# A decoder layer on one core: a unit's weighted values in one step of TensorE, ahead of the products with Wo

## The chip, the cores and the metric

The kernel runs on one core of a Trainium2 chip. The metric is the device time of one execution in microseconds (us). The kernel before took 1291.42 us, the median of three runs (1290.22 to 1291.81). Lower is better.

## The reference

`x` and `ctx` are (8, 256, 1024) float32, that is 8 sequences of 256 tokens. One layer is computed:

```python
qkv = x @ w_qkv                       # 32 query heads, 8 key and 8 value heads of 32
xq, xk = rope(xq), rope(xk)           # four query heads share one key and value head
probs = softmax(where(causal, xq @ xk.T / sqrt(32), -inf))
x = layernorm(x + (probs @ xv) @ w_o)
Q, K = x @ Wq.T + bq, ctx @ Wk.T + bk
x = layernorm(x + softmax(Q @ K.T / sqrt(1024)) @ ctx)
w = dequant_4bit(qweight, lut4)       # bit planes and a table of 16 values a row
x = layernorm(x + x @ w.T + bias)
```

(The third part also has an 8-bit weight for rows whose norm is over 64; rows of a layer norm over 1024 elements have a norm of 32, so the kernel computes the 4-bit product alone.)

Every large product is made from three matmuls: each operand is split into a high part (rounded by ScalarE) and a low part (the difference, by VectorE or GpSimd), and high x high, low x high and high x low are added up.

## The kernel before

There are five stages. Stage 1 (the first 210 us) computes the rotated queries and keys of three groups of 512 tokens in "pairs" of 48 matmuls, the values, and decodes on VectorE the first row blocks of the 4-bit weight; TensorE turns each decoded block (`turn_f`, eight transposes). Stage 2 (210 to some 665 us) is the self attention with the product with Wo. Then come the folding of Wq and Wk, the cross attention and the 4-bit product. The change is in stages 1 and 2.

Stage 2 runs over 8 batches (sequences). A batch is 24 steps (`SUB`), written out by hand on each engine in the same order; batches 0 and 1 stand on their own (age 0 and 1), batches 2 to 7 are a loop (age 2). A unit is one key head with its four query heads and takes three steps. The first two steps hold two heads each, of the later 128 queries against 256 keys; the third holds four heads of the first 128 queries against 128 keys. What happens to the scores of one step, engine by engine:

- TensorE: `scores` (L779) into a bank of PSUM.
- VectorE: `maxima`, masking and the row maximum, head by head (L1562).
- ScalarE: `exponent` (L1187), head by head.
- VectorE: the reciprocal of the sums (L1570), then GpSimd: `scale_probs` (L1907).
- TensorE, three steps later (`LAG`): `turn_probs` (L794, L805), four transposes into one of two banks.
- The copy of that bank to `probT`: by ScalarE for the first and third steps of a unit (L1117 in `probs_out`), by VectorE for the second (L1578). On ScalarE the copy stands behind the exponent of the step that it is in (from batch 1 on).
- TensorE, five steps later than the scores (`PV_LAG`): `weighted` (L818), the product of probabilities and values, in tiles of 32 columns.
- VectorE: the result to `att` (L1587). ScalarE and VectorE split `att`, and TensorE multiplies by Wo one batch later, four matmuls (128x512) in each step (`project_step`, L870).

TensorE's order in a step is: scores, four matmuls with Wo, weighted values, transposes. In batch 0, where no `att` of an earlier batch exists, about 30 matmuls of the last group's queries, keys and values (`fill`) take the place of those with Wo. The weighted values of a unit were issued in two parts: the 8 matmuls of its first two steps in a first step of a later unit (L834) and the 4 matmuls of its third step in the following, a second step (L838). The trace holds two records for each of these matmuls, so 16 and 8.

Each engine works strictly through its own list of instructions. VectorE's list for a second step of a unit is: maxima, reciprocal, copy of `probT`, copy of `att`, and at steps 4 and 16 of a batch the normalising of a 128x1024 tile (L1612, `NORM_STEP`); then the maxima of the third step follow. The tables `WO_STEPS`, `STEPS_OF`, `F_TURN` name the steps at which the parts of Wo are split, parts of the decoding are done and decoded blocks are turned. SyncE issues all DMAs in one order: the load of a unit's queries, keys and values stands behind the stores of the rotated last items (`store_item`).

## Time and profile before

| | |
|---|---|
| median of three runs | 1291.42 us |
| the profiled execution, own time | 1288.92 us |
| its span in the profile | 1287.1 us |
| TensorE matmul busy | 1263.6 us (98%) |
| VectorE, ScalarE, GpSimd busy | 901.6, 531.4, 477.2 us |
| granted TensorE clock | 0.999 |

Matmuls overlap in the records (a 128x512 matmul is recorded with 390 ns and the next starts 230 ns later), so a busy TensorE is read here from where one matmul starts to where the next one does. In rows of a view by time, x4 means that four instructions of one line in a row are shown as one, from the start of the first to the end of the last.

### The profile page before, as it was taken

The numbers are of one execution on the slowest core, as the hardware profiler recorded it, in microseconds if no ns is written. First come the engines' busy times: TensorE is split into PE (matmuls) and PEld (weight loads), VectorE is DVE, ScalarE is ACT, GpSimd is POOL, SyncE is SP. The second block draws the span as 40 slices with busy tenths as digits, with TensorE's granted clock in tenths as the row PEclk, the third lists the DMA queues.
The fourth block names the chain that finished last, engine by engine and source line by source line (L and its number), as shares of the span: only waits on it lengthen the run. The fifth ranks groups of instructions, "written<-read, shape, count | busy, mean of one in ns | idle before, by whom it ended". The sixth has DMA issues, their size and how long they took to land.

```text
span 1287.1 us, 25356 instructions
## 1 busy us (share of the span) xinstructions
PE 1263.6 (98%) x8230; PEld 1041.7 (81%) x8230; DVE 901.6 (70%) x2526; ACT 531.4 (41%) x1597; POOL 477.2 (37%) x413
## 2 busy tenths in 40 slices
PE   8999999998999999999999999999999999999997
PEld 6887888997777777777777887888888888888886
DVE  7999898578888888888876974353443636556665
ACT  4131212457777777777760223243433433100110
POOL 3512122345656656656550000544334450222221
PEclk9999999999999999999999999999999999999999
DMA  7165435463864344344343215125251419212221
GB/s 280 68 213 170 144 132 203 141 208 113 236 182 120 118 134 127 114 135 134 121 127 106 68 34 173 41 82 181 66 196 64 149 49 358 100 65 98 98 87 60
DMA packets 135450, 170.43 MB, mean 132 GB/s; under 512 B 36688, under 2 KB 100176, under 8 KB 134736
## 3 DMA queue, kind: packets, MB, share of 16 engines
q1 hardware_dynamic: 135376, 169.47, 40.6%
q8 instruction: 43, 0.70, 0.2%
q14 instruction: 31, 0.25, 0.1%
HBM read 112.80 MB, written 56.62 MB: 132 GB/s over the span
## 4 chain that ended last, share of the span: by engine, by line
PE 72%; issue 12%; DVE 8%; POOL 4%; SPq 2%; DMA 1%; ACT 1%; POOLq 0%; DVEq 0%; ACTq 0%
PE bank L863 13%; PE bank L677 11%; PE bank L679 11%; PE bank L678 11%; PE bank L805 7%; PE bank L763 4%; PE bank L790 4%; POOL x2b L1984 3%; PE bank L834 3%; PE bank L838 2%; PE bank L726 1%; DVE bits L1482 1%; PE bank L982 1%; DVE pick_b L1521 1%; DVE pick_c L1510 1%
## 5 line engine op out<-in xcount | busy, mean ns | idle before, releaser
L1907 POOL TENSOR_TENSOR prob<-prob,rinv 128x512 f32<-128x512 f32 x192 | 205.5, 1071 | 204.8 <-DVE rinv L1570 204.7
L1187 ACT ACTIVATE prob<-bank,nmax 128x256 f32<-128x256 f32 (+1 forms) x512 | 211.3, 427 | 90.6 <-DVE nmax L1562 83.9
L1562 DVE CUSTOM_DVE_ANT_0 bank<-bank,mask 128x256 f32<-128x256 f32 (+1 forms) x512 | 169.3, 383 | 7.3 <-PE bank L790 3.7
L805 PE MATMUL bank<-ident,prob 128*128 128x128 f32 x768 | 122.0, 282 | 2.8 <-ACT probT L1117 2.8
L805 PEld LDWEIGHTS bank<-ident,prob 128*128 128x128 f32 x768 | 85.4, 141 | 35.9 <-issue 16.7
L1187 ACT ACTIVATION_READ_ACCUMULATOR prob<-bank,nmax 128x1 f32 x512 | 108.1, 211 | 0.0
L1723 DVE SCALAR_TENSOR_TENSOR k_lo<-bank,bA,k_hi 128x512 fp32r<-128x512 f32 x32 | 24.0, 751 | 115.1 <-ACT k_hi L1320 114.5
L790 PE MATMUL bank<-k,q 96*128 96x256 f32 (+1 forms) x512 | 102.8, 303 | 1.7 <-DMA vv<-v_scr 1.7
L863 PE MATMUL bank<-wo_hi,att_hi 128*128 128x512 f32 x256 | 103.9, 406 | 0.0
L677 PE MATMUL bank<-f_hi,x2T_hi 128*128 128x512 f32 x256 | 101.0, 395 | 0.8 <-DVE x2T_lo L1418 0.8
L677 PE MATMUL bank<-cT_hi,m_hi 128*128 128x512 f32 x256 | 100.4, 392 | 0.7 <-DVE cT_lo L1418 0.7
L863 PE MATMUL bank<-wo_hi,att_lo 128*128 128x512 f32 x256 | 101.0, 395 | 0.0
L677 PE MATMUL bank<-xc_hi,w_hi 128*128 128x512 f32 x240 | 94.9, 395 | 5.8 <-DVE xc_lo L1418 5.8
L863 PE MATMUL bank<-wo_lo,att_hi 128*128 128x512 f32 x256 | 100.4, 392 | 0.0
L679 PE MATMUL bank<-f_hi,x2T_lo 128*128 128x512 f32 x256 | 99.8, 390 | 0.0
L679 PE MATMUL bank<-cT_hi,m_lo 128*128 128x512 f32 x256 | 99.7, 390 | 0.0
L678 PE MATMUL bank<-cT_lo,m_hi 128*128 128x512 f32 x256 | 99.6, 389 | 0.0
L678 PE MATMUL bank<-f_lo,x2T_hi 128*128 128x512 f32 x256 | 99.6, 389 | 0.0
L678 PE MATMUL bank<-xc_lo,w_hi 128*128 128x512 f32 x240 | 94.2, 392 | 0.0
L679 PE MATMUL bank<-xc_hi,w_lo 128*128 128x512 f32 x240 | 94.2, 392 | 0.0
L1117 ACT ACTIVATE probT<-bank 128x512 f32<-128x512 f32 x128 | 78.2, 611 | 24.8 <-PE bank L805 24.8
L1944 POOL TENSOR_TENSOR cu<-cx_in,u_bc 128x1024 f32<-128x1024 f32 x16 | 38.4, 2400 | 134.1 <-DMA f_scr<-late_e 119.6
(201 smaller groups left out, 3145.9 us busy)
## 6 DMA issues: line engine op xcount, KB each, us to landing
q<-qk_scr SPq DMA_DIRECT2D x192, 128.0 KB, 2.4
x_st<-x_scr SPq DMA_DIRECT2D x32, 512.0 KB, 3.8
qk_scr<-rot SPq DMA_DIRECT2D x60, 256.0 KB, 2.6
xc_in<-x_cols SPq DMA_DIRECT2D x32, 256.0 KB, 4.7
y<-x SPq DMA_DIRECT2D x16, 512.0 KB, 3.6
x_scr<-y SPq DMA_DIRECT2D x16, 512.0 KB, 2.7
cx_in<-ctx_in SPq DMA_DIRECT2D x16, 512.0 KB, 4.9
x_scr<-x_st SPq DMA_DIRECT2D x16, 512.0 KB, 3.3
```

Of the source, the lines that this page charges most:

```text
L677: nc.tensor.matmul(o, l_hi, r_hi, start=first, stop=False)
L678: nc.tensor.matmul(o, l_hi, r_lo, start=False, stop=False)
L679: return nc.tensor.matmul(o, l_lo, r_hi, start=False, stop=last)
L763: mm = nc.tensor.matmul(o, (w_lo if ps == 2 else w_hi)[:, c, kt, side * P:(side + 1) * P], (x_lo if ps == 1 else x_hi)[:, kt, e * SEQ:(e + ...
L790: mm = nc.tensor.matmul(o[:, i * keys:(i + 1) * keys], q3[slot][:, h, t0:t0 + P], k3[slot][:, 0:keys], start=i == 0, stop=i == len(hs) - 1 ...
L805: mm = nc.tensor.transpose(tb[:, at * P:(at + 1) * P], prob[:, k % 4, c:c + P], ident[:, :])
L834: mm = nc.tensor.matmul(OBANK[HD * h:HD * (h + 1), P:2 * P], v[:, t, :], src, start=t == 0, stop=t == 1, skip_group_check=True)
L863: mm = nc.tensor.matmul(o[:, :], lt[:, kt, st * P:(st + 1) * P], rt[:, kt, half * BANK:(half + 1) * BANK], start=kt == 0 and ps == 0, stop ...
L1117: return nc.scalar.activation(o, i, ACT.Copy)
L1187: mm = nc.scalar.activation(prob[:, k % 4, i * keys:(i + 1) * keys], SBANK[pos][:, i * keys:(i + 1) * keys], ACT.Exp, bias=nmax[:, k % 4, ...
L1562: mm = nc.vector.tensor_tensor_reduce(part, part, mask[:, 2 * P - keys:2 * P], 1.0, BIGGEST, ALU.add, ALU.min, nmax[:, k % 4, i:i + 1])
L1907: nc.gpsimd.tensor_tensor(pr, pr, rinv[:, k % 4, 0:n].unsqueeze(2).to_broadcast([P, n, keys]), ALU.mult)\
```

## The change

Four things change.

1. `weighted` issues all 12 matmuls of a unit in one call, in the second step of a unit, and waits ahead of them for the copies of all three steps. In that step it stands between the scores and the four matmuls with Wo.
2. Six of the eight low parts of Wo are computed by GpSimd in batch 0 instead of by VectorE; the last two stay on VectorE, one step later than before. One high part on ScalarE is a step earlier, two are a step later, and the rotation of the last item is one step later on all engines.
3. In stage 1 the transposes of a decoded block come after 12 matmuls of the following pair instead of ahead of it.
4. The steps of the decoding around the low parts of the next group (`X_LOW_AFTER`) are dealt out by a table.

```diff
             def weighted(b, k):
-                pos, unit = k % 3, k // 3
-                if pos == 0:
+                unit = k // 3
+                if k % 3 < 2:
                     return
-                taken(b, k - 1)
-                taken(b, k)
+                for i in range(3):
+                    taken(b, k - 2 + i)
...
+                wait(pe, att_ready, KVH * b + unit)
+                for t in range(2):
                     for h in range(REP):
-                        mm = nc.tensor.matmul(OBANK[HD * h:HD * (h + 1), 0:P], v[:, 0, :],
-                                              probT[:, k % 4, h * P:(h + 1) * P], start=True, stop=True,
+                        src = probT[:, (k - 2 + h // 2) % 4, (2 * t + h % 2) * P:(2 * t + h % 2 + 1) * P]
+                        mm = nc.tensor.matmul(OBANK[HD * h:HD * (h + 1), P:2 * P], v[:, t, :], src,
+                                              start=t == 0, stop=t == 1, skip_group_check=True)
+                mm.then_inc(pv_done, 1)
+                for h in range(REP):
+                    mm = nc.tensor.matmul(OBANK[HD * h:HD * (h + 1), 0:P], v[:, 0, :],
+                                          probT[:, k % 4, h * P:(h + 1) * P], start=True, stop=True,
...
-                    project_step(b, k, age)
                     if age or k >= PV_LAG:
                         late(b, k - PV_LAG, weighted)
+                    project_step(b, k, age)
                     if age or k >= LAG:
                         late(b, k - LAG, turn_probs)
...
-        WO_STEPS = {(0, 12): 2, (0, 14): 3, (0, 18): 0, (0, 19): 1, (0, 20): 4, (0, 22): 5, (1, 4): 6, (1, 6): 7}
+        WO_STEPS = {(0, 12): 2, (0, 14): 3, (0, 18): 0, (0, 19): 1, (0, 20): 4, (0, 21): 5, (1, 5): 6, (1, 7): 7}
+        X_LOW_AFTER = ((0,) * KT, (2, 2, 3, 3, 4, 4, 5, 5), (2, 2, 3, 3, 4, 5, 5, 6))
...
                 for kt in range(KT):
+                    if turned is not None and kt == TURN_KT:
+                        turn_f(turned)
...
+                    if age == 0 and (0, k - 1) in WO_STEPS:
+                        kt = WO_STEPS[0, k - 1]
+                        pool.wait_ge(wo_hi_ready, WO_TURN[kt] + 1)
+                        nc.gpsimd.tensor_tensor(wo_lo[:, kt, :], wo_in[:, kt, :], wo_hi[:, kt, :].bitcast(F32), ALU.subtract)\
+                            .then_inc(wo_lo_ready, 1)
```

TensorE, the last unit of the loop over batches, from the scores of its second step to those of the third; before (L790 scores, L863 product with Wo, L838 second part of the weighted values, L805 transposes):

```order
L790 MATMUL bank<-k_3,q_3 128x256 [waits exp_done]
L790 MATMUL bank<-k_3,q_3 128x256
L863 MATMUL bank<-wo_hi,att_lo 128x512
L863 MATMUL bank<-wo_hi,att_hi 128x512
L863 MATMUL bank<-wo_lo,att_hi 128x512
L863 MATMUL bank<-wo_hi,att_lo 128x512
L816 REGISTER_ALU [waits pT_dve]
L838 MATMUL bank<-probT,vv 32x128 [waits pT_act]
L838 MATMUL bank<-probT,vv 32x128 x3
L805 MATMUL bank<-ident,prob 128x128 [waits pT_act,prob_ready]
```

and in the changed kernel (L794 scores, L837 and L841 weighted values, L869 product with Wo, L809 transposes):

```order
L794 MATMUL bank<-k_3,q_3 128x256 [waits exp_done]
L794 MATMUL bank<-k_3,q_3 128x256
L820 REGISTER_ALU [waits pT_dve,pT_act]
L837 MATMUL bank<-probT,vv 32x128 [waits att_ready,pT_act]
L837 MATMUL bank<-probT,vv 32x128 x7
L841 MATMUL bank<-probT,vv 32x128 x4
L869 MATMUL bank<-wo_hi,att_lo 128x512
L869 MATMUL bank<-wo_hi,att_hi 128x512
L869 MATMUL bank<-wo_lo,att_hi 128x512
L869 MATMUL bank<-wo_hi,att_lo 128x512
L809 MATMUL bank<-ident,prob 128x128 [waits pT_act,prob_ready]
```

The wait for `pT_act` (ScalarE's copy of the third step's probabilities) moved from behind the four matmuls with Wo to ahead of them; the step before no longer has weighted values.

GpSimd at the end of batch 0, before (L1907 scaling, L1886 and L1887 low parts of a rotated item; the last pair here is item 10, which SyncE stores ahead of a load):

```order
L1907 TENSOR_TENSOR prob<-prob,rinv 128x512 x2
L1886 TENSOR_TENSOR rot_last<-rot_last 128x256
L1887 TENSOR_TENSOR rot_last<-rot_last 128x256
L1907 TENSOR_TENSOR prob<-prob,rinv 128x512 x2
L1886 TENSOR_TENSOR rot_last<-rot_last 128x256
L1887 TENSOR_TENSOR rot_last<-rot_last 128x256
```

and in the changed kernel the same stretch, steps 20 to 23:

```order
L1932 TENSOR_TENSOR wo_lo<-wo_in,wo_hi 128x1024
L1914 TENSOR_TENSOR prob<-prob,rinv 128x512
L1893 TENSOR_TENSOR rot_last<-rot_last 128x256
L1894 TENSOR_TENSOR rot_last<-rot_last 128x256
L1932 TENSOR_TENSOR wo_lo<-wo_in,wo_hi 128x1024
L1914 TENSOR_TENSOR prob<-prob,rinv 128x512
L1932 TENSOR_TENSOR wo_lo<-wo_in,wo_hi 128x1024
L1914 TENSOR_TENSOR prob<-prob,rinv 128x512
L1893 TENSOR_TENSOR rot_last<-rot_last 128x256
L1894 TENSOR_TENSOR rot_last<-rot_last 128x256
```

Low parts of Wo now stand between the scalings and ahead of the last item's rotation.

## Rows read from the trace of the kernel before

**Rows 1.** Stretches: length, busy of PE, PEld, DVE, ACT, POOL; clock, DMA share, GB/s
```profile
210.00:307.20 97.20, 95.60 (x887) 90.94 (x885) 69.30 (x235) 48.53 (x165) 34.85 (x38) 1.00 0.55 168
360.60:660.60 300.00, 300.00 (x2689) 227.23 (x2688) 247.26 (x1115) 229.24 (x900) 175.52 (x168) 1.00 0.42 126
```

**Rows 2.** TensorE by time, one unit of batch 2: start, length, line, operation
```profile
402.53 0.64 PE L790 MATMUL bank<-k,q 96*128 96x128 f32 x4
403.00 0.45 PE L863 MATMUL bank<-wo_hi,att_hi 128*128 128x512 f32 x1
...
403.75 0.39 PE L863 MATMUL bank<-wo_hi,att_hi 128*128 128x512 f32 x1
403.98 0.60 PE L805 MATMUL bank<-ident,prob 128*128 128x128 f32 x4
404.33 0.48 PE L790 MATMUL bank<-k,q 96*128 96x256 f32 x2
...
405.35 0.40 PE L863 MATMUL bank<-wo_lo,att_hi 128*128 128x512 f32 x1
405.68 0.64 PE L834 MATMUL bank<-probT,vv 128*32 128x128 f32 x16
406.25 0.66 PE L805 MATMUL bank<-ident,prob 128*128 128x128 f32 x4
406.66 0.49 PE L790 MATMUL bank<-k,q 96*128 96x256 f32 x2
406.99 0.40 PE L863 MATMUL bank<-wo_hi,att_lo 128*128 128x512 f32 x1
...
408.01 0.43 PE L838 MATMUL bank<-probT,vv 128*32 128x128 f32 x8
408.37 0.65 PE L805 MATMUL bank<-ident,prob 128*128 128x128 f32 x4
408.78 0.64 PE L790 MATMUL bank<-k,q 96*128 96x128 f32 x4
```

**Rows 3.** VectorE in the same unit, in brackets the idle time before
```profile
402.92 0.69 DVE L1578 COPY probT<-bank 128x512 f32<-128x512 f32 x1 [0.36 <-PE bank L805]
403.52 0.41 DVE L1587 COPY att<-bank 128x256 f32<-128x256 f32 x1
403.86 0.29 DVE L1562 CUSTOM_DVE_ANT_0 bank<-bank,mask 128x128 f32<-128x128 f32 x1
```

**Rows 4.** ScalarE by time in the same unit
```profile
404.98 0.37 ACT L1187 ACTIVATE prob<-bank,nmax 128x128 f32<-128x128 f32 x1 [1.22 <-DVE nmax L1562]
...
406.37 0.61 ACT L1117 ACTIVATE probT<-bank 128x512 f32<-128x512 f32 x1
```

**Rows 5.** ScalarE and TensorE at the start of batch 1
```profile
312.19 0.60 ACT L1117 ACTIVATE probT<-bank 128x512 f32<-128x512 f32 x1
...
312.93 0.63 PE L805 MATMUL bank<-ident,prob 128*128 128x128 f32 x4 [1.47 <-ACT probT L1117]
```

**Rows 6.** VectorE by time, from step 4 to step 5 of batch 5
```profile
522.93 0.81 DVE L1612 TENSOR_SCALAR y<-y,mv,rs 128x1024 f32<-128x1024 f32 x1
523.65 0.29 DVE L1562 CUSTOM_DVE_ANT_0 bank<-bank,mask 128x128 f32<-128x128 f32 x1
```

**Rows 7.** Who waited for whom, TensorE: total us, times, longest us
```profile
PE bank L759 <- DVE xc_lo L1418: 1.6, 3, 0.9
PE bank L686 <- DVE pick_a L1521: 1.4, 1, 1.4
```

**Rows 8.** Groups by line: busy us, mean ns, idle before
```profile
L1418 DVE TENSOR_TENSOR wo_lo<-wo_in,wo_hi 128x1024 fp32r<-128x1024 f32 x8 | 11.5, 1432 | 0.8 <-ACT wo_hi L1117 0.8
L1877 POOL TENSOR_TENSOR w_lo<-w_in,w_hi 128x1024 fp32r<-128x1024 f32 x8 | 20.9, 2638 | 23.4 <-ACT w_hi L1117 23.4
```

**Rows 9.** SyncE's queue and TensorE by time, start of batch 1
```profile
314.16 1.82 SPq L425 DMA_DIRECT2D qk_scr<-rot_last  x4
...
322.09 0.51 PE L790 MATMUL bank<-k,q 96*128 96x256 f32 x2 [1.19 <-DMA vv<-v_scr]
```

More of the change, by code:

```diff
@@ L694, in turn_f, with qk_pair @@
                 turn(decode_tiles(b)[1][:, :].bitcast(F32), banks, fps_ready)
-            def qk_pair(g, c):
+            def qk_pair(g, c, turned=None):
                 n = PAIRS * g + c
@@ L730, in values @@
                         mm.then_inc(x_lo_used if low else x_used, 1)
-            for at in ORDER:
+            for i, at in enumerate(ORDER):
                 if at[1] < PAIRS:
-                    qk_pair(*at)
+                    qk_pair(*at, F_TURN.get(ORDER[i - 1]) if i else None)
                 else:
@@ L818, in weighted @@
             def weighted(b, k):
-                pos, unit = k % 3, k // 3
-                if pos == 0:
+                unit = k // 3
+                if k % 3 < 2:
                     return
-                taken(b, k - 1)
-                taken(b, k)
+                for i in range(3):
+                    taken(b, k - 2 + i)
                 v = vv[unit % SLOTS]
-                if isinstance(b, int) and b == 0 and k == 1:
+                if isinstance(b, int) and b == 0 and unit == 0:
                     pe.wait_ge(f_lo_ready, 2 * EARLY)
-                if pos == 1:
-                    wait(pe, att_ready, KVH * b + unit)
-                    for t in range(2):
-                        for h in range(REP):
-                            src = probT[:, (k - 1 + h // 2) % 4, (2 * t + h % 2) * P:(2 * t + h % 2 + 1) * P]
-                            mm = nc.tensor.matmul(OBANK[HD * h:HD * (h + 1), P:2 * P], v[:, t, :], src,
-                                                  start=t == 0, stop=t == 1, skip_group_check=True)
-                else:
-                    for h in range(REP):
-                        mm = nc.tensor.matmul(OBANK[HD * h:HD * (h + 1), 0:P], v[:, 0, :],
-                                              probT[:, k % 4, h * P:(h + 1) * P], start=True, stop=True,
-                                              skip_group_check=True)
+                wait(pe, att_ready, KVH * b + unit)
+                for t in range(2):
+                    for h in range(REP):
+                        src = probT[:, (k - 2 + h // 2) % 4, (2 * t + h % 2) * P:(2 * t + h % 2 + 1) * P]
[5 more added lines that the diff above has]
+                                          probT[:, k % 4, h * P:(h + 1) * P], start=True, stop=True,
+                                          skip_group_check=True)
                 mm.then_inc(pv_done, 1)
@@ L1229, in stage2_batch @@
                         rope_high(item_pair((k - 3) // 2))
-                    if age == 1 and k == 3:
+                    if age == 1 and k == 4:
                         rope_high(item_pair(11))
@@ L1546, in _ @@
                     f_low(F_TURN[g, c])
-                n, end = STEPS_OF[g, c], STEP_END[g, c]
-                for i in range(KT):
-                    if c == PAIRS - 1:
-                        x_low(g + 1, i)
-                    for go in EARLY_STEPS[end - n + n * i // KT:end - n + n * (i + 1) // KT]:
+                steps = EARLY_STEPS[STEP_END[g, c] - STEPS_OF[g, c]:STEP_END[g, c]]
+                marks = [0] + list(X_LOW_AFTER[g]) if c == PAIRS - 1 else [0]
+                for i, at in enumerate(marks):
+                    if i:
+                        x_low(g + 1, i - 1)
+                    for go in steps[at:marks[i + 1] if i + 1 < len(marks) else len(steps)]:
                         go()
@@ L1636, in stage2_batch @@
                         rope_item((k - 2) // 2)
-                    if age == 1 and k == 2:
+                    if age == 1 and k == 3:
                         rope_item(11)
@@ L1640, in stage2_batch @@
                         f_low(EARLY - 1, (OBANK, OBANK), (TURN_LAST[k],))
-                    if age < 2 and (age, k - 1) in WO_STEPS:
+                    if age == 1 and (age, k - 1) in WO_STEPS:
                         kt = WO_STEPS[age, k - 1]
                         dve.wait_ge(wo_hi_ready, WO_TURN[kt] + 1)
-                        low(wo_lo[:, kt, :], wo_in[:, kt, :], wo_hi[:, kt, :]).then_inc(wo_lo_ready, 1)
+                        low(wo_lo[:, kt, :], wo_in[:, kt, :], wo_hi[:, kt, :]).then_inc(wo_lo2_ready, 1)
                     if k in NORM_STEP and NORM_STEP[k][0] <= age:
@@ L1921, in stage2_batch @@
                         rope_low(item_pair((k - 3) // 2))
-                    if age == 1 and k == 3:
+                    if age == 0 and (0, k - 1) in WO_STEPS:
[3 more added lines that the diff above has]
+                            .then_inc(wo_lo_ready, 1)
+                    if age == 1 and k == 4:
                         rope_low(item_pair(11))
```

12 lines of the change are left out of this document (8 added, 4 removed).

## The prediction

> **What bounds the kernel now.** I read the stretches first. In the loop of stage 2 TensorE is busy in 300.00 of 300.00 us [rows 1], at the full clock, against 247 us of VectorE and 229 us of ScalarE. That says who sets the pace, not how much air there is, because a recorded matmul overlaps its successor. So I went to TensorE by time and read starts [rows 2]. A unit, from the scores of one third step to those of the next, takes 408.78 - 402.53 = 6.25 us, as 300 us for 48 units do. Its steps are 1.80 us (third), 2.33 (first) and 2.12 (second). The reader is to see two bubbles there: from a matmul with Wo to the next operation takes 0.23 us when that is a transpose (403.75 to 403.98), but 0.33 when it is a weighted value (405.35 to 405.68); and four transposes take 0.35 us behind a matmul with Wo (403.98 to 404.33) but 0.41 behind weighted values (406.25 to 406.66).
>
> Then I asked what each weighted value waits for, and this is where the change is decided. ScalarE copies the third step's turned probabilities behind the exponent of the step it is in, and that is again a third step, the one with four heads. The chain in this unit: the transposes end and VectorE copies `probT` at 402.92, which it had waited for [rows 3]; it copies `att` at 403.52 and can begin the maxima at 403.86, although the scores began at 402.53. ScalarE waits 1.22 us for the maxima and begins the exponents at 404.98; its copy starts at 406.37 and ends at 406.98 [rows 4]. That is 4.45 us behind the scores of that step. Before, the weighted values that need it came at 408.01 [rows 2], 1.03 us later: the air was hidden there, behind four matmuls with Wo.
>
> **The change: what it takes away.** Merging the 8 records into the block of 16. The second part costs, behind a product with Wo: 0.33 us to its start, 0.36 to the transposes (408.01 to 408.37), and 0.41 for these; without it 0.23 and 0.35. So 1.10 - 0.58 = 0.52 us go. In the joined block its 8 records cost some 0.22 (16 records take 0.57 to the transposes, 8 take 0.36, so 8 more cost 0.21) [rows 2]. That leaves 0.3 us a unit; I take 0.28 since starts are rounded. Putting the block ahead of the product instead of behind only moves the bubbles: scores to block instead of product to block, block to product instead of block to transposes.
>
> The Trainium skill (TensorEngine Tiling (Array Packing), Key Properties) says that a change of tiling mode drains TensorE. The 0.33 against 0.23 us agree with it. By that rule alone the change would save its 0.3 us for each of 64 units; that is the first rival below.
>
> **What it adds.** The joined block now waits for the copy right behind the scores of the second step. Without any wait that step would begin 1.80 + 1.60 = 3.40 us behind the third step's scores: 1.80 as now, and the first step with no weighted values in it is 2.33 less (0.33 + 0.57 + 0.41) plus (0.23 + 0.35), that is 1.60. The two scores take 0.33 to what follows (406.66 to 406.99) and 0.10 more for the other tile shape, so TensorE would be at the block 3.83 us behind the third step's scores. The copy ends at 4.45. The change takes 1.03 us of air and moves the block 1.65 us forward: TensorE must wait some 0.6 us, plus the time from the copy's end to the start of what it releases. Where TensorE did wait for such a copy, that was 312.93 - (312.19 + 0.60) = 0.14 us [rows 5]. Nothing of ScalarE's or VectorE's lists in this chain is changed, so 4.45 stays: its first link is the end of the transposes of the second step, and those move with TensorE.
>
> Behind the waiting block stand the four matmuls with Wo, which do not need it, the transposes, and the next scores; then VectorE waits for these transposes, which starts the chain again. So the period of a unit becomes this loop: 4.45 (scores to the copy's end) + 0.14 + the block. The block to the product: 0.57 + 0.22 = 0.79. The product to the transposes, with the first matmul not preloaded: 0.98 (403.00 to 403.98), and 0.35 for the transposes. Sum 4.45 + 0.14 + 0.79 + 0.98 + 0.35 = 6.71, against 6.25. I take +0.47 a unit, as the first matmul of 512 columns may hide a little less. Bounds: +0.35 if the release takes only 0.02, +0.52 if that first matmul hides nothing.
>
> The loop has lost its air, so what VectorE does in it now counts in full. Between the copy of `att` and the maxima of the third step stands the normalising at steps 4 and 16 of a batch. It holds the maxima by 523.65 - 522.93 = 0.72 us [rows 6]. Twice in each of batches 2 to 7 and once in batch 1: 13 x 0.72 = 9.4 us. From below 3 us (if the backlog that it causes is caught up with elsewhere), from above 12 us (if the adding and the splitting of `att` come into the loop too). I find about 1 us of free VectorE time in a unit of 6.7 us for those, so I take 9.4.
>
> Units in the loop: 48 in batches 2 to 7, and some 6 of batch 1: 54 x 0.47 = 25.4 us (bounds 19 to 28).
>
> In batch 0 the steps are some 4 us long (`fill` comes ahead of the block in both), the copy is ready long before, and the merging gains: six units x 0.28 = -1.7 us.
>
> Stage 1: TensorE waits 1.4 us for the first decoded block, once [rows 7]; 12 matmuls ahead of the transposes cover that. But TensorE then waits 1.6 us for VectorE's low parts at the start of batch 0 in the same rows: VectorE carries that stretch, and it gets the transposed block later, not earlier. I take 0, between -1.4 and +1.
>
> Low parts of Wo: six leave VectorE (1.43 us each) and cost GpSimd 2.64 each, the price of the same shape for `w_lo` [rows 8], 15.8 us in all. GpSimd is busy 34.85 of 97.20 us there [rows 1], which hides them as a whole. But four stand among the last four steps, ahead of the last items' rotation. SyncE stores such an item at 314.16, the load behind it is what TensorE waits for at 322.09 [rows 9]. VectorE being freer, its reciprocals release GpSimd earlier; adding up GpSimd's list from step 19 on I come out at about the same 314. I take 0, from -1.5 to +6. The other moves of a step (high parts, last rotation) go with it.
>
> Sum: 25.4 + 9.4 - 1.7 = +33.1 us. Against the profiled execution's own 1288.92 us that is 1322.0; the median of the runs lies 2.5 us above it, and on 1291.42 it gives 1324.5 us. With all bounds on one side, 1291.4 + 19 + 3 - 1.7 - 2.9 = 1309 and 1291.4 + 28 + 12 - 1.7 + 7 = 1337.
>
> **Rivals.** First, the intended gain: the copy is no bound, because ScalarE finds its work earlier when TensorE is quicker. Then 64 x 0.28 = 18 us go, 1273 us. For it: TensorE is 100% busy and the others are at 82% and less [rows 1]. Against it: the 1.22 us that ScalarE waits in rows 4 end with VectorE's maxima, and these start with TensorE's own transposes; nothing in the chain can start earlier.
>
> Second, a partial one: the chain shortens by some half microsecond (shorter instructions with less contention, an earlier release), so that the gain of merging and the wait cancel, some 1291 us. I see no row for it.
>
> Third, on the side of slower still: GpSimd does not finish the low parts ahead of the last rotation. Each is 2.64 us, and from the moment that GpSimd runs without a pause from step 19 on, each that is not covered holds SyncE's list and TensorE's scores of batch 1 by as much. With two uncovered 5.3 us more, about 1330. For it: four of them in four steps. Against: 62 us of idle time in the stretch.
>
> Fourth, the merging saves nothing, as both parts of the block have their own waits and write other columns: 0.28 x 54 more in the loop, about 1341. Against it: both have the same tile shape, and no wait stands between them now.
>
> A rule that bears on the first: the Trainium skill (TensorE: Matmul & The Clock Gate, Part 3, The mechanism) says that matmuls keep their program order and only weight loads are pulled ahead. By it the product with Wo can't fill the wait, and the +33 us stand; with it free to pass, the first rival's time would come out. In rows 5 no matmul from behind the waiting transposes started in their 1.47 us; the trace agrees.
>
> **How the numbers follow.** Forecast (the loop binds) 76%, intended gain 8%, cancelling 5%, GpSimd 8%, no merging gain 3%. A measurement of this kernel can't tell less than about 0.2% (2.6 us) from no change. Faster: the first rival and a part of the second, 0.10. Same: 0.02. Slower: 0.88. The range 1303 to 1341 holds the forecast with its bounds, the third and most of the fourth rival, and leaves the first two out, with a few per cent for a gentler loop.
>
> **What would show it.** In the loop of stage 2: a unit of about 6.7 us (6.0 for the first rival); TensorE idle some 0.7 us ahead of the weighted values in each unit, put down to ScalarE's copy of `probT`, 30 to 45 us in all; the copy's end still about 4.45 us behind the third step's scores; one bubble of 0.1 us less at the transposes; units with a normalising longer by 0.7 us. TensorE's busy time in the 300 us falls below 100%. Stage 2 ends some 33 us later, everything behind it keeps its length. If ScalarE's copy ends under 3.9 us behind the scores, the forecast's central step is wrong.

## The result, and the profile after

The changed kernel takes 1319.33 us (median of four runs, 1318.53 to 1320.70) against 1290.82 us for the kernel before beside it (1289.05 to 1291.81). The ratio is 1.0216, 95% interval 1.0202 to 1.0229: slower by 28.5 us. The forecast was 1324.5 us, range 1303 to 1341.

The profiled execution of the changed kernel took 1318.53 us, 29.6 more than that of before (1288.92). Its page begins with the busy time of each engine:

```profile
span 1316.7 us, 25356 instructions
PE 1250.0 (95%) x8230; PEld 1056.6 (80%) x8230; DVE 895.7 (68%) x2520; ACT 530.9 (40%) x1597; POOL 490.6 (37%) x419
```

Where the 29.6 us arise is read from five starts of scores on TensorE (L790 before, L794 after; start and length come first): the first and the fourth step of batch 0, the first steps of batches 1 and 2, and the last step of stage 2. In the kernel before:

```profile
210.97 0.40 PE L790 MATMUL bank<-k,q 96*128 96x256 f32 x2
223.00 0.28 PE L790 MATMUL bank<-k,q 96*128 96x256 f32 x1
307.18 0.36 PE L790 MATMUL bank<-k,q 96*128 96x256 f32 x1
360.55 0.36 PE L790 MATMUL bank<-k,q 96*128 96x256 f32 x1
658.93 0.31 PE L790 MATMUL bank<-k,q 96*128 96x128 f32 x1
```

and after:

```profile
210.45 0.40 PE L794 MATMUL bank<-k,q 96*128 96x256 f32 x2
220.01 0.28 PE L794 MATMUL bank<-k,q 96*128 96x256 f32 x1
302.45 0.36 PE L794 MATMUL bank<-k,q 96*128 96x256 f32 x1
359.14 0.36 PE L794 MATMUL bank<-k,q 96*128 96x256 f32 x1
687.62 0.30 PE L794 MATMUL bank<-k,q 96*128 96x128 f32 x1
```

| stretch | before | after | difference | forecast |
|---|---|---|---|---|
| stage 1 | 210.97 | 210.45 | -0.5 | 0 |
| first three steps of batch 0 | 12.03 | 9.56 | -2.5 | 0 |
| rest of batch 0 | 84.18 | 82.44 | -1.7 | -1.7 |
| batch 1 | 53.37 | 56.69 | +3.3 | 6 x 0.47 + 0.72 = +3.5 |
| batches 2 to 7 | 298.38 | 328.48 | +30.1 | 48 x 0.47 + 12 x 0.72 = +31.2 |
| from the last scores to the end | 628.2 | 629.1 | +0.9 | 0 |

The stretch in which the forecast put the loss holds it. Against the second line of [rows 1], where TensorE was busy in all of 300 us, the changed kernel has here (length, busy of PE, PEld, DVE, ACT, POOL, clock, DMA share, GB/s)

```profile
360.00:660.00 300.00, 264.66 (x2447) 217.81 (x2446) 225.92 (x1012) 209.60 (x823) 159.46 (x153) 1.00 0.38 115
```

at the same clock: TensorE is idle in 35 us, and every other engine is less busy too. The waits point at one circle through TensorE, VectorE and ScalarE (us in total, times, longest); e2, e3 and e8 below test it:

```profile
ACT prob L1193 <- DVE nmax L1569: 112.5, 74, 2.5
DVE probT L1585 <- PE bank L809: 63.7, 60, 2.8
PEld bank L837 <- ACT probT L1123: 56.0, 56, 1.6
PE bank L837 <- ACT probT L1123: 44.7, 55, 1.4
```

The last line is new: TensorE ahead of the joined block, 55 of 64 times. (The line above it is the loading of weights for the same matmuls, a record of its own, `PEld`.) One unit of the loop, TensorE by time from the scores of the third step to those of the next (compare [rows 2]):

```profile
433.21 0.64 PE L794 MATMUL bank<-k,q 96*128 96x128 f32 x4
...
435.02 0.48 PE L794 MATMUL bank<-k,q 96*128 96x256 f32 x2
...
436.62 0.48 PE L794 MATMUL bank<-k,q 96*128 96x256 f32 x2
437.71 0.64 PE L837 MATMUL bank<-probT,vv 128*32 128x128 f32 x16 [0.61 <-ACT probT L1123]
438.18 0.40 PE L841 MATMUL bank<-probT,vv 128*32 128x128 f32 x8
438.51 0.50 PE L869 MATMUL bank<-wo_hi,att_lo 128*128 128x512 f32 x1
...
439.54 0.60 PE L809 MATMUL bank<-ident,prob 128*128 128x128 f32 x4
439.90 0.64 PE L794 MATMUL bank<-k,q 96*128 96x128 f32 x4
```

and ScalarE in it (compare [rows 4]):

```profile
435.67 0.37 ACT L1193 ACTIVATE prob<-bank,nmax 128x128 f32<-128x128 f32 x1 [1.46 <-DVE nmax L1569]
...
437.06 0.61 ACT L1123 ACTIVATE probT<-bank 128x512 f32<-128x512 f32 x1
```

The reader is to see the steps of 1.81, 1.60 and 3.28 us; the copy that ends at 437.67, which is 4.46 us behind the third step's scores; and the block that starts 0.04 us later (0.05 in 48 of the kernel's 64 blocks). The four matmuls with Wo behind it need nothing from the copy and still wait with it. In e3 below, without a wait, this step takes 2.59 us (409.64 to 412.23).

### The profile page after: what moved, and what is told of

The parts are those of the page before. It is cut to its first block, busy times and chain, and to the rows that moved or that the text cites. A ratio compares the mean times of both kernels' runs of the same rounds, so it can differ in the third digit from the quotient of the medians.

```text
span 1316.7 us, 25356 instructions
## 1 busy us (share of the span) xinstructions
PE 1250.0 (95%) x8230; PEld 1056.6 (80%) x8230; DVE 895.7 (68%) x2520; ACT 530.9 (40%) x1597; POOL 490.6 (37%) x419
## 4 chain that ended last, share of the span: by engine, by line
PE 65%; issue 15%; ACT 8%; DVE 6%; POOL 4%; DMA 1%; SPq 0%; ACTq 0%; DVEq 0%; POOLq 0%
PE bank L681 13%; PE bank L683 13%; PE bank L682 13%; PE bank L869 7%; ACT prob L1193 6%; PE bank L767 4%; PE bank L837 3%; POOL x2b L1996 3%; PE bank L732 3%; PE bank L809 3%; DVE bank L1569 3%; ACT probT L1123 2%; PE bank L794 2%; DVE nmax L1569 1%; DVE att L1594 1%
## 5 line engine op out<-in xcount | busy, mean ns | idle before, releaser
L809 PE MATMUL bank<-ident,prob 128*128 128x128 f32 x768 | 115.3, 273 | 3.7 <-POOL prob L1914 2.5
L809 PEld LDWEIGHTS bank<-ident,prob 128*128 128x128 f32 x768 | 94.2, 140 | 28.8 <-POOL prob L1914 5.2
L869 PE MATMUL bank<-wo_hi,att_lo 128*128 128x512 f32 x256 | 106.6, 416 | 0.0
L794 PE MATMUL bank<-k,q 96*128 96x256 f32 (+1 forms) x512 | 102.5, 302 | 1.4 <-DMA vv<-v_scr 1.4
L869 PE MATMUL bank<-wo_hi,att_hi 128*128 128x512 f32 x256 | 103.6, 405 | 0.0
L869 PE MATMUL bank<-wo_lo,att_hi 128*128 128x512 f32 x256 | 101.1, 395 | 0.0
L1585 DVE COPY probT<-bank 128x512 f32<-128x512 f32 x64 | 44.2, 691 | 65.5 <-PE bank L809 63.7
```

What stands on the lines that cost most here:

```text
L794: mm = nc.tensor.matmul(o[:, i * keys:(i + 1) * keys], q3[slot][:, h, t0:t0 + P], k3[slot][:, 0:keys], start=i == 0, stop=i == len(hs) - 1 ...
L809: mm = nc.tensor.transpose(tb[:, at * P:(at + 1) * P], prob[:, k % 4, c:c + P], ident[:, :])
L869: mm = nc.tensor.matmul(o[:, :], lt[:, kt, st * P:(st + 1) * P], rt[:, kt, half * BANK:(half + 1) * BANK], start=kt == 0 and ps == 0, stop ...
L1585: nc.vector.tensor_copy(probT[:, k % 4, :], TBANK[k % 2][:, :]).then_inc(pT_dve, 1)
```

## The experiments

All times are medians. Ratios are against runs of the kernel before taken beside them, whose median lies between 1290.20 and 1291.20 us, with the 95% interval; they are estimated from all runs and can differ in the third decimal from the quotient of two medians. "Batch of the loop" is the distance between two batches' scores in batches 2 to 7, "clean unit" the commonest length of three steps.

| kernel | us | ratio | batch of the loop | clean unit |
|---|---|---|---|---|
| before | 1290.8 | 1 | 50.03 | 6.25 |
| changed | 1319.3 | 1.0216 | 55.07 | 6.68 |
| e1 joined block ahead, alone | 1324.3 | 1.0263 | 55.04 | 6.68 |
| e2 joined block behind Wo | 1283.9 | 0.9949 | 49.63 | 5.95 |
| e3 ScalarE's copy first | 1278.3 | 0.9901 | 48.55 | 5.99 |
| e4 two parts ahead of Wo | 1301.3 | 1.0084 | 52.21 | 6.35 |
| e5 turns only | 1289.5 | 0.9992 | 50.03 | 6.25 |
| e6 decoding order only | 1288.5 | 0.9977 | 50.03 | 6.25 |
| e7 low parts of Wo only | 1289.1 | 0.9991 | 50.03 | 6.25 |
| e8 normalising a step later | 1309.8 | 1.0147 | 53.57 | 6.68 |
| e9 = e2 and e3 | 1276.1 | 0.9893 | 48.31 | 5.95 |
| e10 = e3 and e8 | 1275.6 | 0.9886 | 48.35 | 5.99 |
| e11 = e3, loads of unit 4 first | 1278.5 | 0.9909 | 48.54 | 5.99 |
| e12 = e2, e3, e8 and the loads | 1273.2 | 0.9862 | 48.05 | 5.95 |

### e1: the joined block alone

The kernel before with the first of the four changes:

```diff
-                taken(b, k - 1)
-                taken(b, k)
+                for i in range(3):
+                    taken(b, k - 2 + i)
...
-                    project_step(b, k, age)
                     if age or k >= PV_LAG:
                         late(b, k - PV_LAG, weighted)
+                    project_step(b, k, age)
```

> The kernel before with the first edit alone: the joined block of weighted values, ahead of the product with Wo. Loop theory (the wait for ScalarE's copy closes a loop through TensorE's transposes, VectorE and ScalarE): the whole loss is in this edit, and the 3 us that the changed kernel gained by the start of batch 0 go, so 1290.8 + 28.5 + 3 = 1322 us, units of 6.68 us in the loop of stage 2. Rival (the low parts of Wo on GpSimd hold up batch 1 and what follows): some 1291 us.

Measured 1324.29 us (1321.50 to 1324.57), ratio 1.0263 (1.0246 to 1.0280), with batches of 55.04 us and units of 6.68 and 7.40. The whole loss is in this edit. From the fourth step of batch 0 to batch 1 it takes 82.46 us instead of 84.18: the merging does give 1.7 us where nothing waits for the copy. In its trace the fourth step of batch 0 starts 3.1 us later than in the changed kernel (223.09 against 220.01) and the last scores 3.0 us later (690.59 against 687.62), so the changed kernel keeps to the end of stage 2 what its other edits win at the start.

### e2: the joined block behind the product with Wo

The changed kernel with the one line moved back:

```diff
+                    project_step(b, k, age)
                     if age or k >= PV_LAG:
                         late(b, k - PV_LAG, weighted)
-                    project_step(b, k, age)
```

> The changed kernel with the joined block back behind the four matmuls with Wo. Loop theory: TensorE is at the block 3.40 + 0.33 + 0.70 + 0.33 = 4.76 us behind the third step's scores, the copy is ready at 4.45 + 0.05, so no wait, and a unit is TensorE's own 5.97 us; 54 units x 0.71 = 38 us less than the changed kernel. The 13 units with a normalising wait some 0.46 instead of 0.72 us: 3 us less. About 1278 us. Rival (the joined block itself costs time, by its change of tile shape or its three waits, wherever it stands): no less than 1291 us.

Measured 1283.88 us (1282.12 to 1284.92), ratio 0.9949 (0.9932 to 0.9966). One unit of it, TensorE by time:

```profile
404.06 0.64 PE L794 MATMUL bank<-k,q 96*128 96x128 f32 x4
...
407.48 0.48 PE L794 MATMUL bank<-k,q 96*128 96x256 f32 x2
407.80 0.40 PE L869 MATMUL bank<-wo_hi,att_lo 128*128 128x512 f32 x1
...
408.81 0.64 PE L837 MATMUL bank<-probT,vv 128*32 128x128 f32 x16
409.27 0.40 PE L841 MATMUL bank<-probT,vv 128*32 128x128 f32 x8
409.61 0.66 PE L809 MATMUL bank<-ident,prob 128*128 128x128 f32 x4
410.02 0.64 PE L794 MATMUL bank<-k,q 96*128 96x128 f32 x4
```

and ScalarE's copy:

```profile
407.90 0.61 ACT L1123 ACTIVATE probT<-bank 128x512 f32<-128x512 f32 x1
```

The copy ends at 408.51, again 4.45 us behind the third step's scores, and the block comes 0.30 us later without a wait. So the merging gives its 0.3 us (6.25 to 5.95), and the four matmuls with Wo are cover again. But 0.30 us of air is less than a normalising: in each batch one unit takes 6.47 and one 7.08 us, and a batch 49.63 instead of 8 x 5.95 = 47.6. TensorE still waits for the copy 10.1 us in 14 places (44.7 in the changed kernel). The unit of 6.47 is close to the 0.46 us that was forecast for a normalising. In that of 7.08 the copy ends 5.82 us behind the scores (515.38 and 521.20): VectorE has the adding, the statistics and a low part of `att` from 511.91 to 514.36, comes late to the maxima behind them, and then has the normalising too. That is 0.67 us a batch more than forecast, and two units beside it are 0.16 and 0.20 us longer than clean: some 6 us over six batches, by which it missed its 1278.

### e3: ScalarE's copy ahead of the exponents

The changed kernel, batches 1 to 7, third steps only:

```diff
+                    elif k % 3 == 2:
+                        late(b, k - LAG, probs_out)
+                        exponent(b, k)
                     else:
                         exponent(b, k)
```

> The changed kernel, with ScalarE's copy of the third step's probabilities ahead of the four exponents of its step instead of behind them (batches 1 to 7). Loop theory: the copy ends some 2.5 us behind the third step's scores instead of 4.45, TensorE reaches the block at 3.83 and does not wait, units of 5.97 us, a normalising is no longer in the loop: 1319.3 - 54 x 0.71 - 13 x 0.72 = 1272 us. Rival (TensorE loses the time by the change of tile shape between scores, block and product): 1319 us, as nothing on TensorE moves.

Measured 1278.31 us (1276.14 to 1279.35), ratio 0.9901 (0.9884 to 0.9917). ScalarE and TensorE in one unit whose third step's scores start at 406.24:

```profile
408.40 0.60 ACT L1123 ACTIVATE probT<-bank 128x512 f32<-128x512 f32 x1 [0.69 <-PE bank L809]
408.90 0.36 ACT L1193 ACTIVATE prob<-bank,nmax 128x128 f32<-128x128 f32 x1
```

```profile
406.24 0.64 PE L794 MATMUL bank<-k,q 96*128 96x128 f32 x4
...
409.64 0.48 PE L794 MATMUL bank<-k,q 96*128 96x256 f32 x2
410.05 0.65 PE L837 MATMUL bank<-probT,vv 128*32 128x128 f32 x16
```

The copy ends 2.76 us behind the scores instead of 4.46, and the block begins 1.05 us after it with the product still behind: TensorE's wait for this copy shrinks from 44.7 to 0.9 us over the kernel, and that one wait is the last block's, behind the loop. This turns 28.5 us of loss into 12 us of gain with nothing but the place of one instruction on another engine. It misses the 1272 us by 6. Reckoned from the changed kernel's span, 1316.7 - 47.7, its own span of 1277.5 is 8.5 us too long: 3.5 are a wait for a load in batch 1 that e11 looks at, 3.3 (0.55 a batch) are units of 6.31 and 6.22, and 1.7 are TensorE's clock, which stood at half from 334.7 to 338.1 us, right behind that wait (see the last section). The same edit in the kernel before, without the joined block, was not tried.

### e4: two parts, both ahead of the product

The changed kernel with `weighted` as before (8 matmuls in a first step, 4 in a second step), called ahead of `project_step`:

```diff
-                for i in range(3):
-                    taken(b, k - 2 + i)
+                taken(b, k - 1)
+                taken(b, k)
...
+                if pos == 1:
                     wait(pe, att_ready, KVH * b + unit)
```

> The changed kernel with the weighted values in two parts as before, but both ahead of the product with Wo. Loop theory: the loop is then 4.45 + 0.05 + 0.36 (8 records) + 1.02 + 0.35 = 6.23 us, just TensorE's own 6.25, so a clean unit is as before, and only the 13 normalisings come on top: 1290.8 - 3 + 9.4 = 1297 us. Rival (place ahead of the product costs as such, by change of tile shape): 1319 us or more, since there are then more such changes than in the changed kernel.

Measured 1301.30 us (1300.41 to 1302.52), ratio 1.0084 (1.0067 to 1.0100). The second part of a unit and its copy:

```profile
407.02 0.48 PE L794 MATMUL bank<-k,q 96*128 96x256 f32 x2
407.43 0.43 PE L842 MATMUL bank<-probT,vv 128*32 128x128 f32 x8
407.79 0.50 PE L870 MATMUL bank<-wo_hi,att_lo 128*128 128x512 f32 x1
```

```profile
406.65 0.61 ACT L1124 ACTIVATE probT<-bank 128x512 f32<-128x512 f32 x1
```

The first part now stands ahead of the copy too and fills most of the gap: the copy ends at 407.26, the part starts at 407.43 without a wait. A clean unit takes 6.35 us, 0.10 more than before, of which 0.07 are in the step with the 16 records (2.40 us against 2.33): the bubbles at the changes of tile shape are a little dearer at this place; and the normalising comes through (units of 6.97 and 7.09), since only 0.17 us of air is left. The time lies nearer to the 1297 of the loop than to the 1319 that the place of the wait alone would give, and 48 x 0.10 us are the difference to 1297: what decides is how much work stands ahead of the block.

### e5, e6, e7: the other three changes alone

Each is the kernel before with one change. In e5 the turning stands behind 12 of the 48 matmuls of the pair, as in the changed kernel:

```diff
# e5
+                    if turned is not None and kt == TURN_KT:
+                        turn_f(turned)
# e6
+        X_LOW_AFTER = ((0,) * KT, (2, 2, 3, 3, 4, 4, 5, 5), (2, 2, 3, 3, 4, 5, 5, 6))
# e7, on GpSimd in batch 0
+                        nc.gpsimd.tensor_tensor(wo_lo[:, kt, :], wo_in[:, kt, :], wo_hi[:, kt, :].bitcast(F32), ALU.subtract)\
+                            .then_inc(wo_lo_ready, 1)
```

> The kernel before with nothing of the change but the turning of the decoded block inside a pair (behind two of its sixteen matmul groups) instead of behind the pair. In the traces the changed kernel begins the first scores of batch 0 0.5 us earlier (210.45 against 210.97) and reaches its fourth step another 2.5 us earlier. Theory A: the turn takes part of TensorE's one wait of 1.4 us for the decoded block, and nothing else: first scores at 210.5, about 1290.3 us, which a measurement hardly tells from no change. Theory B: the turns are what brings the whole 3.0 us: fourth step at 220.0, about 1287.8 us.

> The kernel before with nothing of the change but the order on VectorE in the last pair of a group of stage 1: two decoding operations ahead of the first low part of x instead of a low part first. In the trace of before VectorE stands idle for 2.38 us at 202.8 to 205.2 ahead of such a low part, which waits for ScalarE's high part; in the changed kernel a decoding operation of 1.41 us stands there (203.67), and VectorE's first maxima of batch 0 begin at 216.28 instead of 219.42. Theory A: this order alone brings those 2.5 to 3 us: fourth step of batch 0 at about 220.3 instead of 223.0, time about 1288 us. Theory B (it is the turns): 223.0 and 1290.8 us as before.

> The kernel before with nothing of the change but six of the eight low parts of Wo on GpSimd instead of VectorE, at the same steps. Theory A (as predicted): VectorE loses 8.6 us of work that is not on the path in batch 0, GpSimd gains 15.8 us that fit in its idle time: 1290.8 us, within 1.5. Theory B: the last items' rotation is held up on GpSimd, SyncE's store of item 10 comes later than 314.16 and so the first scores of batch 1: up to 1296 us. Theory C: VectorE is the bound of some steps of batch 0, so that these become shorter and 2 to 4 us go: 1287 to 1289 us.

The medians of eleven runs are 1289.51, 1288.53 and 1289.10 us against 1290.20 (27 runs): ratios 0.9992 (0.9983 to 1.0001), 0.9977 (0.9967 to 0.9986) and 0.9991 (0.9982 to 1.0000). Only the second interval leaves out 1; by its median e6 is 1.7 us quicker, by its ratio 3.0. The traces say which does what. With the turns alone, the first scores come at 210.35 and the fourth step at 222.37, 0.6 us earlier: TensorE's 1.4 us of [rows 7] for the decoded block are gone, and its 1.6 us for the low parts stay. The 0.6 us are small against the scatter of that start, but it holds over the traces: without this edit the first scores come at 210.93 to 211.17 (four traces), with it at 209.88 to 210.87 (ten). With the decoding order alone the 1.6 us go and the 1.4 stay; the fourth step starts at 220.73, 2.3 us earlier. VectorE in the kernel before stood idle ahead of the first low part, since ScalarE's high part was not there:

```profile
205.17 0.69 DVE L1418 TENSOR_TENSOR xc_lo<-xc_in,xc_hi 128x512 fp32r<-128x512 f32 x1 [2.38 <-ACT xc_hi L1117]
```

and in e6 two decoding operations stand in that gap, which before came later, among the low parts that TensorE waited for:

```profile
202.91 1.38 DVE L1522 COPY_PREDICATED pick_b<-bits,pick_c 128x1024 int32<-128x1024 int32 x1
204.39 1.42 DVE L1522 COPY_PREDICATED pick_a<-bits,pick_b 128x1024 int32<-128x1024 int32 x1
205.69 0.68 DVE L1419 TENSOR_TENSOR xc_lo<-xc_in,xc_hi 128x512 fp32r<-128x512 f32 x1
```

Both theories A hold at the start of batch 0. Little of the lead seems left later: batch 3 starts in the three traces at 411.43, 410.31 and 410.88 against 410.59. That is mostly the clock. In each of these three traces TensorE's granted clock falls to 0.50 for some 3.4 us early in batch 1 (from 322.2, 321.1 and 316.9), which costs up to half of that, 1.7 us, and in that of the kernel before it does not. Of e6's 2.3 us some 2.0 are left without it, in keeping with the medians. The low parts of Wo on GpSimd change nothing that can be told from no change. SyncE's store of item 10 starts at 312.62, earlier than the 314.16 of before, which speaks against theory B, and batch 0 from its fourth step takes 84.19 us against 84.18, which speaks against C. They take 2.40 us each in batch 0 (2.37 to 2.41) instead of the 2.64 that was taken for them.

### e8: both normalisings one step later

```diff
-        NORM_STEP = {16: (1, 0), 4: (2, 1)}
+        NORM_STEP = {17: (1, 0), 5: (2, 1)}
```

> The changed kernel with both normalisings of a batch one step later on VectorE (steps 5 and 17 instead of 4 and 16), which puts them behind the maxima of a third step instead of ahead of them. Theory of the loop: they leave the loop (third step's scores, maxima, exponents, copy, block); the 13 units that last 7.41 us become 6.68, 13 x 0.72 = 9.4 us go, about 1310 us. Rival: VectorE has no air in these units wherever the 0.72 us stand, they come back one unit later: 1319 us, with units of 7.4 us still there.

Measured 1309.83 us (1308.87 to 1311.04), ratio 1.0147 (1.0131 to 1.0162): 9.5 us less than the changed kernel. All units with a normalising are at 6.68 us, and a batch takes 53.57 instead of 55.07. In the changed kernel VectorE had

```profile
371.74 0.41 DVE L1594 COPY att<-bank 128x256 f32<-128x256 f32 x1
372.07 0.81 DVE L1619 TENSOR_SCALAR y<-y,mv,rs 128x1024 f32<-128x1024 f32 x1
372.79 0.29 DVE L1569 CUSTOM_DVE_ANT_0 bank<-bank,mask 128x128 f32<-128x128 f32 x1
```

and TensorE then waited for the copy of this unit 1.35 us instead of 0.61. This is the same 0.72 us as in [rows 6], where it cost nothing. With the normalising behind the four maxima instead of ahead of them the wait is 0.60. VectorE's busy time is the same (895.3 against 895.7 us); only what stands in the circle counts. In the kernel before the cover was all but used up in one unit of each batch of the loop, where the copy ended only 0.05 us ahead of the part that needs it.

### e9, e10, e11, e12: what is left, and the best version

> The changed kernel with ScalarE's copy of the third step's turned probabilities ahead of that step's four exponents, and the joined block behind the product with Wo. Either edit alone gave 1278 and 1284 us, with clean units of 5.99 and 5.95 us. Theory: with the copy ahead the loop has more than 1 us of air, so that where the block stands no longer counts and TensorE's own 5.97 us a unit are the floor; the block behind the product gives the units of the first edit that are not clean (6.31 and 6.22) some air. All units 5.95 to 6.05, about 1275 us. Rival: the place of the block counts by itself, by the order of tile shapes on TensorE: then the clean units differ from 5.99 by more than 0.1.

> The changed kernel with ScalarE's copy ahead of the exponents, and both normalisings one step later (steps 5 and 17). With the copy ahead the maxima of the third step no longer stand in the chain that releases the block; the normalising stood ahead of these maxima. Theory A: it therefore costs nothing any more and moving it gains nothing: 1278 us. Theory B: the units of 6.31 and 6.22 us are the normalising's, 0.5 us a batch go: 1275 us.

> The changed kernel with ScalarE's copy ahead of the exponents, and in SyncE's list of batch 1 the loads of unit 4 ahead of the first block of wq and the first block of x instead of behind them (for this the high and low parts of wq stand three steps later on ScalarE and GpSimd). With the copy ahead TensorE waits 3.5 us at 330.2 us for the values of unit 4, which were issued at 326.48 and landed 7 us later. Theory: that wait is a queue behind the two transfers of 512 KB; with the loads ahead they land by 328 us and the wait goes, 3.5 us: 1275 us. Rival: TensorE runs ahead of the loads in batch 1 anyway and waits at the next unit instead: 1278 us.

> The changed kernel with all four edits of the experiments: joined block behind the product with Wo, ScalarE's copy ahead of the third step's exponents, normalisings one step later, and in batch 1 the loads of unit 4 ahead of those of wq and x. From the traces: the batches of the loop take 48.35 us with copy and normalising, and 48.31 with copy and block behind; of their 6.32 or 6.37 us for one unit in eight neither edit touched the cause, of the 6.22 the normalising was it. Both together: 8 units of 5.95 and 0.37 more for one, 47.97 us a batch, 6 x 0.38 = 2.3 us less than with copy and normalising alone; the loads of unit 4 gave 2.3 us at the end of batch 1 in the trace, and no difference in the times. Theory A: both add up, 1275.6 - 2.3 - 2.3 = about 1271 us. Theory B: the loads only shift the wait to later units of batch 1, 1273.3 us. Rival: nothing of it adds, 1275.6 us.

e9 is e3 with e2's line moved: 1276.14 us, ratio 0.9893 (0.9874 to 0.9911), units of 5.95, and still 6.37 and 6.22 in each batch. The place of the block, 5.99 against 5.95, hardly counts any more; that all units would come to 5.95 to 6.05 did not hold. e10 is e3 with e8's numbers: 1275.58 us, ratio 0.9886 (0.9869 to 0.9902). The unit of 6.22 goes, that of 6.32 stays, so of the two only one was the normalising's: half of theory B. The rest of its gain is in batch 1, which is 2.8 us shorter: its wait for the values of unit 4 is 2.23 us instead of 3.49, with the loads in the same order as in e3, and it has no fall of the clock there. Nothing shows that the edit did either. e11 is e3 with the high and low parts of wq three steps later and

```diff
+                load_unit(b, 4)
                 if age == 1:
-                    load_wq((0,))
...
-                    load_y1(0, 0)
-                load_unit(b, 4)
-                if age == 1:
+                    load_wq((0,))
+                    load_y1(0, 0)
```

In e3 TensorE waited in batch 1 for the loads of two units (start, length, and in brackets the idle time before):

```profile
318.19 0.50 PE L794 MATMUL bank<-k,q 96*128 96x256 f32 x2 [2.22 <-DMA vv<-v_scr]
333.94 0.51 PE L794 MATMUL bank<-k,q 96*128 96x256 f32 x2 [3.49 <-DMA vv<-v_scr]
```

In e3 the values of unit 4, issued at 326.48, land at 333.89. In e11 they are issued at 326.19, ahead of the blocks of 512 KB, and land at 328.52: the wait was the queue, as the theory had it. Four waits of 0.17 to 0.55 us at the following units stand in its place:

```profile
318.97 0.50 PE L794 MATMUL bank<-k,q 96*128 96x256 f32 x2 [2.99 <-DMA vv<-v_scr]
337.51 0.50 PE L794 MATMUL bank<-k,q 96*128 96x256 f32 x2 [0.27 <-DMA vv<-v_scr]
...
357.29 0.49 PE L794 MATMUL bank<-k,q 96*128 96x256 f32 x2 [0.55 <-DMA vv<-v_scr]
```

Batch 2 starts at 357.29 instead of 359.56, but the time is 1278.54 us (ratio 0.9909, 0.9893 to 0.9926), no different from 1278.31 and the number of the rival. Of these 2.3 us 1.7 are the fall of the clock in e3 at 334.7 us, which e11 does not have there, so the loads bring some 0.6. In the profiled run of e11 the same fall comes behind stage 2: from 760 to 800 us the mean granted clock was 0.96 (e3 1.00, both with TensorE busy in 39.33 of the 40 us). With one fall each the two traces end 0.7 us apart. e12, with all four edits, gives 1273.23 us (1271.21 to 1274.03), ratio 0.9862 (0.9846 to 0.9878), 18.0 us less than before. The median is the number of theory B. Between the traces of e12 and e10, neither of which has a fall of the clock ahead of its last 5 us, there are 3.7 us, 1.9 of them in batch 1 and 1.8 in the loop; that is nearer to theory A, so the two are not told apart. Its batches take 48.05 us against the 47.97 expected. The one unit of 6.38 us left in a batch is no wait for the block. VectorE spends 505.49 to 507.94 on the adding, the statistics and the low part of `att` ahead of the maxima of the next step,

```profile
505.49 0.66 DVE L1611 TENSOR_TENSOR y<-bank,y 128x512 f32<-128x512 f32 x1
...
507.94 0.42 DVE L1572 CUSTOM_DVE_ANT_0 bank<-bank,mask 128x256 f32<-128x256 f32 x1
```

and the exponents, and with them the copy behind them in that step, come late; TensorE's transposes at 510.40 wait for that copy.

## Why the prediction was right, point by point

**The circle.** Forecast 4.45 + 0.14 + 0.79 + 0.98 + 0.35 = 6.71 us a unit. Measured in the unit shown: 4.46 from the scores to the copy's end, 0.04 to the block, 0.80 from the block to the product, 1.03 to the transposes and 0.36 to the next scores, 6.69; the commonest unit is 6.68. That the copy's end stays at 4.45 us while TensorE moves was the central step, and it holds in the changed kernel and in e2. The mis-sized term is the release: 0.14 us was read from the transposes of [rows 5]; the block starts 0.04 to 0.05 us after the copy. The first matmul of 512 columns hides 0.05 less than it was given, so that 0.43 us a unit came out for 0.47.

**Nothing passes the waiting block.** The product with Wo never filled the gap; e2 and e3, which give the block's wait cover or shorten it, show that this is worth 35 to 41 us. The rule of the Trainium skill on program order (TensorE: Matmul & The Clock Gate, Part 3, The mechanism) held: for all 56 blocks in the steps of batches 1 to 7 the record ahead of the block is that of the scores, never a product with Wo. The first rival had the right size for the merging, 0.3 us a unit, and the wrong condition.

**The normalising.** 0.72 us forecast. The two units of a batch that hold one take 7.41, 0.73 over the clean 6.68, and e8 takes 9.5 us away where 9.4 were forecast. The adding and the splitting, which were taken to fit in the air, stand ahead of the one unit of a batch that takes 0.16 us more (6.83 or 6.84); no run moved them.

**Batch 0.** -1.7 forecast, -1.74 measured, and e1 gives it alone; e4, with the two parts again, takes 84.18 us for this stretch, as before.

**The edits that were set to nothing.** This is where the forecast's +33.1 and the measured +29.6 part: the start of batch 0 brings 3.0 us, forecast 0 with -1.4 as its lower end. The failed step is "VectorE carries that stretch, and it gets the transposed block later, not earlier": VectorE did carry it, but it had 2.38 us of idle time just ahead, and the new table fills this with decoding. The third change was weighed there and the fourth, the one that acted more, was not. e5 and e6 split the 3.0 us into 0.6 and 2.3. Low parts of Wo at 0: e7 agrees. SyncE's store of item 10, which the third rival wanted later than 314.16, starts at 309.84 in the changed kernel, 7.4 us behind the first scores of batch 1 where it was 7.0 before:

```profile
309.84 1.82 SPq L429 DMA_DIRECT2D qk_scr<-rot_last  x4
```

The rest is +0.9 us from the last scores on, and 1.3 us too much for batches 1 to 7. The 0.9 us are the circle's last turns, which the sum over batches left out: behind the last scores TensorE waits for ScalarE's copy 1.17 and 0.89 us (0.41 and 0.20 before), and the last block ends 9.25 us behind these scores instead of 8.28. The 1.3 us are 54 x 0.04 = 2.2 us too much for the circle, less the 0.16 us of six units that were taken to fit in the air. The three other edits together are worth 3.0 us between the traces of e1 and the changed kernel, neither with a fall of the clock in stage 2, and 5.0 between their medians; of e1's four runs three had a lower mean clock (0.997 and 0.998) than the one traced (0.999).

## What to carry to other kernels

Ahead of moving a consumer forward in an in-order list, find where its producer ends, counted from an event that moves with the consumer, and compare that with where the consumer would stand; the work between them is the cover, and a busy share of 100% does not say how much of it there is. When the wait closes a circle through other engines, everything in the circle costs its full length in every turn: either keep independent work ahead of the wait, or move the producer's instruction forward on its own engine, which here took 41 us from the changed kernel, where the merging gives 0.3 us a unit at best. And a difference of 1 or 2 us between two traces is not an effect of an edit until the granted clock has been compared in short stretches: here one fall of it was as large as three of the effects looked for.

## What was not expected of the hardware

A matmul that waited for ScalarE's copy started 0.04 to 0.05 us after the copy's recorded end when its tile was the 32-column one (48 blocks of the changed kernel), while transposes took 0.14 (three times in the kernel before, once in the changed one).

The granted clock fell to 0.50, the lower of its two levels (1.2 instead of 2.4 GHz), for some 3.4 us at a time, at different places in different traces: from 318.4 us in e2, 334.7 in e3, 804.6 in e4, 322.2 in e5, 321.1 in e6, 316.9 in e7, 308.8 in e8, 308.4, 332.3 and 779.4 in e9, and 781.6 in e11. In those of the kernel before, the changed kernel, e1, e10 and e12 it did not, before the last 6 us. Where TensorE sets the pace one fall costs 1.7 us, half its length: a 128x512 matmul started every 0.43 us in it instead of every 0.23 (e11).

The falls in batch 1 came within 1 us of the end of a wait of TensorE (1.31 us in e5, 1.60 in e6, 3.49 in e3), but the changed kernel and e10 had such waits of 1.76 us without a fall. The three late ones, in e4, e9 and e11, came 0.9 to 1.3 us behind the end of four matmuls of two rows each, in a stretch in which TensorE was recorded busy without a pause (in e9 and e11 since 700 us); e3 has the same work there and no fall. So what brings it about is open. It makes up part of the scatter of the runs: of the 27 runs of the kernel before beside e5 to e8, three with a mean clock of 0.999 took 1288.3 to 1288.8 us and four with 0.996 took 1291.2 to 1291.6.

The same subtraction of 128x1024 on GpSimd took 2.40 us in batch 0 and 2.64 in stage 1 [rows 8]; the cause was not tried.

A load of 32 KB behind loads of 512 KB in SyncE's list took 7.4 us from issue to landing in e3 (326.48 to 333.89) and 2.3 in e11, where it was issued at the same time but ahead of them; its median is 2.1. With the order of e3 it took 4.8 us in the changed kernel and 6.2 in e10, so the size of such a wait differs from one trace to the next.
